# Layer-3 attention: its first chunks prepared in the stage ahead, and the output written by chunk

## The reference

```python
h = silu((n @ w1_w.T) * w1_s) * ((n @ w2_w.T) * w2_s)      # n = layernorm(x)
h = gelu((h @ h1_w.T) * h1_s)
h = gelu((h @ h2_w.T) * h2_s)
x = x + 0.5 * ((h @ w3_w.T) * w3_s)
q, k, v = heads(n @ W_q.T), heads(n @ W_k.T), heads(n @ W_v.T)   # n = layernorm(x), 16 heads of 8
attn = softmax(q @ k.T / sqrt(8))                          # within each batch of 256 tokens
x = x + (attn @ v) @ W_o.T
# and the feed-forward once more
```

## Time and profile before

| what | us |
|---|---|
| three runs | 2952.84 median (2946.71 to 2954.22) |
| the profiled execution | 2956.47 |
| its span | 2954.8 |
| mean granted clock of PE in it | 0.848 of 2.4 GHz |

### The profile page before, as it was taken

One profiled execution on the slowest core, in us unless ns is written; L12 is line 12 of the kernel. 1 busy time (PEld: TensorE's weight loads), 2 busy tenths in 40 slices (PEclk: granted clock), 3 DMA queues, 4 the chain that ended last, 5 costly groups with the idle time before them and its releaser, 6 DMA issues. The chain is left out here.

```text
span 2954.8 us, 44130 instructions
## 1 busy us (share of the span) xinstructions
PE 2255.7 (76%) x13104; PEld 1635.6 (55%) x13105; DVE 1790.6 (61%) x4185; ACT 1048.2 (35%) x2484; POOL 850.4 (29%) x771
## 2 busy tenths in 40 slices
PE   4979959767376732474999951776999699989998
PEld 3645546547364630464666631664877445547777
DVE  5757957573477348841355578725565578855655
ACT  1433315341044101253544412542333156653332
POOL 2544525437404741475000010772000122200000
PEclk9989959965596556798999985997999789989999
DMA  6120011246605567256222263552000233310001
GB/s 209 39 62 1 1 38 39 66 172 133 169 1 179 124 175 143 62 117 146 53 59 52 50 155 61 118 113 70 0 0 0 65 76 94 97 24 1 0 0 29
DMA packets 283584, 221.00 MB, mean 75 GB/s; under 512 B 103072, under 2 KB 254093, under 8 KB 280365
## 3 DMA queue, kind: packets, MB, share of 16 engines
q1 hardware_dynamic: 249261, 185.09, 23.0%
q0 software_dynamic: 34176, 34.09, 7.1%
HBM read 152.98 MB, written 65.17 MB: 74 GB/s over the span
## 5 line engine op out<-in xcount | busy, mean ns | idle before, releaser
L162 POOL TENSOR_TENSOR fields<-ln_t,power 128x4 f32<-128x4 f32 x96 | 98.4, 1051 | 601.0 <-DVE ln_t L155 601.0
L3124 DVE TENSOR_REDUCE s_mx<-s_sa 128x2 f32<-128x512 f32 x256 | 166.6, 686 | 59.8 <-PE s_sa L3277 58.6
L3205 ACT ACTIVATE s_e<-s_sc 128x512 f32<-128x512 f32 x256 | 149.8, 600 | 103.0 <-PE s_sc L3293 100.1
L2860 PE MATMUL s_z<-s_t,s_mix_h 128*128 128x256 f32 x768 | 171.0, 379 | 0.0
L1997 POOL DMA_INDIRECT acc_dram<-s_yo,s_to_i x96 | 152.5, 1588 | 51.8 <-issue 28.1
L1985 POOL DMA_INDIRECT s_xg<-rows_dram,s_from_i x96 | 94.5, 984 | 223.0 <-DVE s_to_i L2118 195.0
L2860 PEld LDWEIGHTS s_z<-s_t,s_mix_h 128*128 128x128 f32 x768 | 145.9, 190 | 19.8
L3277 PE MATMUL s_sa<-s_kx,s_qx 72*128 72x256 bf16 x512 | 110.7, 303 | 26.3 <-DMA s_qx<-q_dram 19.1
L2302 PE MATMUL s_hu<-s_xgt,s_w 128*128 128x128 f32 x768 | 118.6, 301 | 12.4 <-issue 11.5
L191 PE MATMUL s_tp<-ident,xn 128*128 128x128 f32 x192 | 40.3, 347 | 108.0 <-DVE xn L181 106.0
L2906 PE MATMUL s_z<-xnt,s_wt_w 128*128 128x512 f32 x256 | 117.9, 615 | 1.5 <-ACT xnt L197 1.5
(11 more groups left out here) (526 smaller groups left out, 5993.6 us busy)
## 6 DMA issues: line engine op xcount, KB each, us to landing
s_w<-in_L_ffn_W_dram SPq DMA_DIRECT2D x96, 256.0 KB
acc_dram<-s_zero SPq DMA_DIRECT2D x32, 512.0 KB, 5.8
s_share<-share_dram SPq DMA_DIRECT2D x32, 512.0 KB, 6.1
s_kx<-k_dram SPq DMA_DIRECT2D x16, 576.0 KB
s_qx<-q_dram SPq DMA_DIRECT2D x48, 192.0 KB
fields<-acc_dram SPq DMA_DIRECT2D x16, 512.0 KB, 7.5
table_dram<-s_table_rows SPq DMA_DIRECT2D x2, 3136.0 KB, 9.2
s_wg<-in_L_ffn_w_gate_dram SPq DMA_DIRECT2D x64, 96.0 KB
```

Of the source, the lines that this page charges most:

```text
L162: pool.tensor_tensor(core.rstd[:, tiles], core.ln_t[:, 2, tiles], core.power[:, 0:CT], ALU.pow).then_inc(s.scale_ready.sem, 1)
L2860: last = pe.matmul(bank(n)[:, o, :], weights[:, f, o * P:(o + 1) * P], src[:, f, :], start=f == 0, stop=f == HALF - 1)
L3124: dve.tensor_reduce(mx[:, i, t, 2 * pairs:2 * pairs + 2], sa[:, n % 2, :, :], AX.X, ALU.max).then_inc(max_done.sem, 1)
L3205: act.activation(e[:, n % RING, :, :], sc[:, n % 2, :, :], ACT.Exp).then_inc(exp_done.sem, 1)
```

## The change

The parts of layer-3 attention that come ahead of its loop for chunks 0 and 1 go into the first `l3_ffn`, into its last two chunks, 6 and 7 (`first` and unrolled). `early(c, k, at)` is called in each engine's stream between the products of hidden layer k, at point `at`. Chunk 0 of the attention is prepared in chunk 6 (layer 0: scales, normalising, two weights turned, x turned; layer 1: K and Q projections and splitting), chunk 1 in chunk 7 (x turned where the layer norm of a next chunk would be, projections and splitting in layer 0, the last part in layer 1). On PE the two weights are turned after the second product, x after the seventh, K is projected after the third and Q after the sixth product. On ACT the first cut to bf16 follows the first (K) and third (Q) gelu, the second cut the second and fourth. The last of the three parts, and the remainders, are DVE's. PE and ACT use the bank of the layer norm, `s.tp`, and the SBUF of `all_xn`. SP of this stage reads the weights, stores the parts and reads slots 0 and 1, which with the four raw weights (`L3Ahead`) outlive the stage; at its end it waits for all of them.

In the attention the row scores come first. Semaphores of the slots and of the stored parts are preset as if the work had been done there. Chunks 0 and 1 still get their layer norm, for V. The maxima of batch 0 are placed ahead of layer norm, and the 8 row scores of batch 1 are in two halves with V of chunk 0 between them. Three matmuls whose result nobody reads (`warm`) are added, two ahead of the loop and one in batch 0. POOL clears `vz` after two of its eight scales. `warm`, the waits and the order are in the diff.

In the second `l3_ffn` SP writes each chunk of the output as soon as it is added, the statistics of x are not taken, and the stage `end` is gone.

```diff
+class L3Ahead:
+    def __init__(self, s):
+        self.TERMS = 3
+        self.BLOCK = self.TERMS * DH
+        self.ROWS = self.TERMS * self.BLOCK
+        self.ALL_ROWS = self.ROWS + self.TERMS
+        self.NAMES = ("W_q", "W_k", "W_v", "W_o")
+        self.kx = s.sb("kx", [self.ALL_ROWS, 2, HEADS, N], BF16)
+        self.qx = s.sb("qx", [self.ALL_ROWS, 2, HEADS, N], BF16)
+        self.raw = {m: s.sb(f"raw_{m}", [P, P]) for m in self.NAMES}
+def load_operands(eng, core, ahead, slot, kx, qx, sem):
+    eng.dma_start(kx[0:ahead.ROWS, :, :].rearrange("r h t -> r (h t)"),
+                  core.k_dram[slot].rearrange("a d h t -> (a d) (h t)").unsqueeze(1).to_broadcast([ahead.BLOCK, ahead.TERMS, HEADS * N])).then_inc(sem, 16)
+    for a in range(ahead.TERMS):
+        eng.dma_start(qx[a * ahead.BLOCK:(a + 1) * ahead.BLOCK, :, :].rearrange("r h t -> r (h t)"),
+                      core.q_dram[slot].rearrange("d a h t -> (d a) (h t)")).then_inc(sem, 16)
...
+        if first:
+            @block.sync
+            def _(sp):
+                for n, m in enumerate(("W_k", "W_q")):
+                    sp.dma_start(raw_a[n], w[f"L3_attn_{m}"]).then_inc(aw_loaded.sem, 16)
+                for m in ahead.NAMES:
+                    sp.dma_start(ahead.raw[m][:, :], w[f"L3_attn_{m}"]).then_inc(ahead_loaded.sem, 16)
+                for a in range(EARLY):
+                    for n in range(2):
+                        sp.wait_ge(a_split_done.sem, a_split_done.past(2 * a + n))
+                        for i in range(2):
+                            cut = parts[:, n, :, i * N:(i + 1) * N]
+                            if n == 0:
+                                sp.dma_start(core.k_dram[2 * a + i].rearrange("a d h t -> (d h) a t"), cut).then_inc(a_stored[0].sem, 16)
+                            else:
+                                for k in range(TERMS):
+                                    sp.dma_start(core.q_dram[2 * a + i, :, k, :, :], cut[:, k, :]).then_inc(a_stored[1].sem, 16)
+                    if a == 0:
+                        sp.wait_ge(a_stored[0].sem, 32)
+                        sp.wait_ge(a_stored[1].sem, 32 * TERMS)
+                        for i in range(2):
+                            load_operands(sp, core, ahead, i, ahead.kx[:, i, :, :], ahead.qx[:, i, :, :], ahead_loaded.sem)
+                sp.wait_ge(ahead_loaded.sem, 16 * (len(ahead.NAMES) + 2 * (1 + TERMS)))
+                sp.wait_ge(a_stored[0].sem, 32 * EARLY)
+                sp.wait_ge(a_stored[1].sem, 32 * TERMS * EARLY)
...
+        if not first:
+            @block.sync
+            def _(sp):
+                out_rows = core.out.rearrange("b (n p) d -> p (b n) d", p=P)
+                for c in range(CHUNKS):
+                    tiles = slice(c * CT, (c + 1) * CT)
+                    sp.wait_ge(x_added.sem, x_added.past(c))
+                    sp.dma_start(out_rows[:, tiles, :], core.x[:, tiles, :]).then_inc(out_stored.sem, 16)
+                sp.wait_ge(out_stored.sem, 16 * CHUNKS)
...
+            def early_left(a, n):
+                dve.wait_ge(a_first_cut.sem, a_first_cut.past(2 * a + n))
+                dve.scalar_tensor_tensor(left[n], s.tp[:, 0, :], SCALE if n else 1.0, parts[:, n, 0, :],
+                                         ALU.mult, ALU.subtract).then_inc(a_left_ready.sem, 1)
+            def early_last(a, n):
+                dve.wait_ge(a_second_cut.sem, a_second_cut.past(2 * a + n))
+                dve.tensor_tensor(parts[:, n, 2, :], left[n], parts[:, n, 1, :], ALU.subtract).then_inc(a_split_done.sem, 1)
+            def early(c, k, at):
+                if not first or not isinstance(c, int):
+                    return
+                a = c - (CHUNKS - EARLY)
+                if a == 0 and k == 0:
+                    if at == 0:
+                        early_scales()
+                    if at == 3:
+                        early_normal(0, range(2))
+                    if at == 4:
+                        early_normal(0, range(2, CT))
+                if (a, k) in ((0, 1), (1, 0)):
+                    if at == 2:
+                        early_left(a, 0)
+                    if at == 4:
+                        early_last(a, 0)
+                    if at == 5:
+                        early_left(a, 1)
+                if a == 0 and k == 1 and at == 6:
+                    early_last(0, 1)
+                if a == 1 and k == 1 and at == 0:
+                    early_last(1, 1)
...
+                elif first:
+                    early_normal(1)
...
-                dve.wait_ge(x_added.sem, x_added.past(c))
-                new_sums_dve(dve, core, c)
+                if first:
+                    dve.wait_ge(x_added.sem, x_added.past(c))
+                    new_sums_dve(dve, core, c)
...
+            def early_xnt(a):
+                act.wait_ge(a_turned.sem, a_turned.past(a))
+                act.activation(xta, s.tp[:, 0, :], ACT.Copy).then_inc(a_xnt_ready.sem, 1)
+            def early_cut(a, n):
+                act.wait_ge(a_projected.sem, a_projected.past(2 * a + n))
+                if a:
+                    act.wait_ge(a_stored[n].sem, (32, 32 * TERMS)[n] * a)
+                act.activation(parts[:, n, 0, :], s.tp[:, 0, :], ACT.Copy, scale=SCALE if n else 1.0).then_inc(a_first_cut.sem, 1)
+            def early_cut2(a, n):
+                act.wait_ge(a_left_ready.sem, a_left_ready.past(2 * a + n))
+                act.activation(parts[:, n, 1, :], left[n], ACT.Copy).then_inc(a_second_cut.sem, 1)
...
+            def early_turn(a):
+                pe.wait_ge(a_xn_ready.sem, a_xn_ready.past(a))
+                if a:
+                    pe.wait_ge(a_left_ready.sem, a_left_ready.past(2 * a - 1))
+                else:
+                    pe.wait_ge(aw_kept.sem, 1)
+                for j in range(CT):
+                    last = pe.transpose(s.tp[:, 0, j * P:(j + 1) * P], xa[:, j, :], core.ident[:, :])
+                last.then_inc(a_turned.sem, 1)
+            def early_project(a, n):
+                if n:
+                    pe.wait_ge(a_left_ready.sem, a_left_ready.past(2 * a))
+                else:
+                    pe.wait_ge(a_xnt_ready.sem, a_xnt_ready.past(a))
+                pe.matmul(s.tp[:, 0, :], wt_a[n], xta, start=True, stop=True).then_inc(a_projected.sem, 1)
...
-        parts_stored = [s.sig(f"parts_stored{n}", (32, 96)[n]) for n in range(2)]
-        kq_loaded = [s.sig(f"kq_loaded{n}") for n in range(SLOTS)]
+        parts_stored = [s.sig(f"parts_stored{n}", 3 * (32, 96)[n]) for n in range(2)]
+        kq_loaded = [s.sig(f"kq_loaded{n}", (64, 64, 0, 0)[n]) for n in range(SLOTS)]
...
             sp.wait_ge(ones_ready.sem, 1)
-            sp.dma_start(kx[ROWS:ALL_ROWS, :, :, :].rearrange("p u h t -> p (u h t)").rearrange("p (n t) -> p n t", t=CW),
-                         ones[:, :].unsqueeze(1).to_broadcast([TERMS, SLOTS * HEADS * N // CW, CW])).then_inc(ones_loaded.sem, 16)
-            store(0, 0)
-            load(0, 0, 0, False)
-            load(0, 0, 1, False)
-            store(1, 1)
+            for part in (ahead.kx, kx_more):
+                sp.dma_start(part[ROWS:ALL_ROWS, :, :, :].rearrange("p u h t -> p (u h t)").rearrange("p (n t) -> p n t", t=CW),
+                             ones[:, :].unsqueeze(1).to_broadcast([TERMS, 2 * HEADS * N // CW, CW])).then_inc(ones_loaded.sem, 16)
             load(1, 1, 0, False)
             place_nm(0, 0, 0)
...
-            ln_scales_pool(pool, core, s)
-            pool.wait_ge(s.xn_ready.sem, s.xn_ready.past(1))
+            ln_scales_pool(pool, core, s, range(2))
             pool.memset(vz[:, :, :, :, :], 0.0).then_inc(v_clear.sem, 1)
             pool.wait_ge(v_clear.sem, 1)
             pool.memset(vz[:, :, :, :, DH:HW].rearrange("p u j h c -> p (u j h) c"), 1.0).then_inc(v_clear.sem, 1)
             pool.memset(zero[:, :], 0.0).then_inc(v_clear.sem, 1)
             pool.wait_ge(v_clear.sem, 3)
+            ln_scales_pool(pool, core, s, range(2, CHUNKS))
...
+            ln_scales_dve(dve, core, s)
             dve.memset(ones[:, :], 1.0).then_inc(ones_ready.sem, 1)
             dve.memset(m3[:, :, :, TERMS:, :], 0.0)
             dve.tensor_copy(ident_b[:, :], core.ident[:, :]).then_inc(ident_ready.sem, 1)
-            ln_scales_dve(dve, core, s)
-            ln_dve(dve, core, s, 0, 0)
-            ln_dve(dve, core, s, 1, 1)
-            split(0, 0)
-            split(0, 1)
-            split(1, 0)
-            split(1, 1)
-            dve.wait_ge(v_clear.sem, 2)
-            keep_v(0, 0)
             for n in range(STEPS):
                 largest(0, 0, n)
             split_maxima(0)
-            for n in range(LEAD):
+            ln_dve(dve, core, s, 0, 0)
+            for n in range(LEAD // 2):
+                largest(1, 1, n)
+            dve.wait_ge(v_clear.sem, 2)
+            keep_v(0, 0)
+            ln_dve(dve, core, s, 1, 1)
+            for n in range(LEAD // 2, LEAD):
...
+            keep_nm(0, 0)
```

(51 more changed lines are left out.)

189 lines of the change are left out of this document (138 added, 51 removed).

## The result

The median went from 2952.75 us (2946.71 to 2954.22) to 2911.47 us (four runs, 2906.64 to 2916.07): 41.3 us less where 29.6 were forecast. The ratio with its 95% interval, which is not that of the two medians, is 0.9872 [0.985, 0.9893], some 38 us. Two further measurements of the unchanged pair gave 0.9877 [0.9854, 0.9899] and 0.99 [0.9871, 0.9928].

A forecast was written before the change was run, and what follows sets the result against it. PE was taken to bound the feed-forward stage and the attention loop, at a low clock in batch 0. Terms summed to -29.6 us: 2956.5 to 2926.9, less 3.6 for the median, 2923 us; 8-in-10 range 2908 to 2940.

The forecast's parts named there:

- Preparation in chunks 6 and 7: First layer-3 feed-forward stage: added projections and transposes on PE cost +4.6 us (4.6 to 9); DVE and ACT work hidden.
- Rival B: Feed-forward stage ahead pays more, by early steps waiting or an end waiting for stores: up to +8, 2931 us; chance 0.12.
- Stage start: Start of attention: three more SP semaphore increments ahead of the barrier cost +0.2 us (0 to 0.4).
- The prologue: Attention ahead of its loop: first matmul at T + 30.5 instead of T + 50.6, -20.1 us (-22 to -16).
- The row's bound of +3.5: Attention prologue: POOL's memset might hold DVE's maxima, as it held a CAST; bounds 0 and +3.5 us, 0 taken.
- Batch 0: First 16 loop steps of attention: clock raised by warm matmuls, 16 us against 24.05, -8.0 us (-9.2 to +1.7).
- Rival A: Attention loop: the clock stays low through batch 0, whose term becomes +1.7, total 2933 us; chance 0.17.
- The wait for slot 0's second load: Attention loop: PE's wait for chunk 2's operands grows from 1.34 to 2.2 us, +0.9 (0 to 4).
- The output: Tail: stores by chunk leave only a last 256 KB store, landing at 2947.2 instead of 2954.4, -7.2 us (-8 to -5).
- rival C: Attention loop, chunk 6: no fall of the clock after the load wait, 9 us less, 2914 us; chance 0.15.

The follow-up runs named there:

- norm_first: Changed kernel with layer norm of both chunks and chunk 0's V product put back ahead of the maxima: 2911.26 us, ratio 0.9872 to the kernel before.
- no_warm: Changed kernel without its three warm matmuls: 2920.68 us, ratio 0.9907 to the kernel before.
- before_warm: Kernel before with only the three warm matmuls added: 2939.67 us, ratio 0.9964 to the unchanged kernel before.
- before_out: Kernel before with only the output part of the change (stores by chunk, no last statistics, no stage `end`): 2944.26 us, ratio 0.9978.
- both: Changed kernel with Q parts stored as split, row scores and maxima moved forward, one warm matmul ahead of the loop: 2908.11 us, ratio 0.9857 to before.

## Why the prediction was right, point by point

- **Preparation in chunks 6 and 7** (+4.6): +4.5 over the two chunks. Over the whole stage it is 294.9 to 296.6 us in the ten executions with this code against 290.8 to 291.4 in the four without, +4.5 between the means. None of the hand-overs cost anything, and the stage end did not wait for SP: its reads were issued at 2280.9 to 2285.7, 28 us before the end of the last addition, its last stores 6.8 us before. Rival B did not come.
- **Stage start** (+0.2): the gap is 1.67 against 1.64 us. The sum left out the gap ahead of the second feed-forward stage, which went from 1.17 to 1.58; it is part of "the rest".
- **The prologue** (-20.1): -20.3, with the maxima at T + 2.1 and the loop at T + 30.26. T + 30.5 was taken between two sums, T + 31 with the warm matmuls at the low clock and T + 29 with the clock up; the clock was still low, and the work ahead of them 0.7 shorter than summed. The memset held nothing: 13 maxima took 9.05 us, 0.696 each, against the 0.69 of the earlier trace rows. The row's bound of +3.5, from the CAST, did not apply to a reduction from PSUM. The Trainium skill's "SBUF — State Buffer" ("Who interferes with whom") names no reduction among the operations that can take the shared port pair, and the trace agrees. norm_first adds what the sum had not separated: only 1.8 of these 20 us are the order.
- **Batch 0** (-8.0): -8.7. Two microseconds were taken as low; it was 0.9 (2346.6 to 2347.5). no_warm and before_warm, one from each side, confirm the cause: 23.55 without the warm matmuls, 15.06 with them. Rival A did not come.
- **The wait for slot 0's second load** (+0.9): here the step failed. The prediction had PE's way get 0.9 shorter and the chain from K's projection to the landing keep its length. But that 0.9 is the K projection itself, which stands in both. The first cut on POOL, which follows it, before and after:

```profile
2394.21 1.04 POOL L3090 TENSOR_TENSOR s_parts<-s_proj,s_zero 128x512 bf16<-128x512 f32 x1 [60.73 <-ACT s_proj L3200]
...
2362.27 1.04 POOL L3324 TENSOR_TENSOR s_parts<-s_proj,s_zero 128x512 bf16<-128x512 f32 x1 [32.86 <-ACT s_proj L3421]
```

It starts 3.64 us after K's projection did, and now 2.54: 1.1 of the chain went with the clock. The whole chain was 2420.32 - 2390.57 = 29.75 and is 2387.70 - 2359.73 = 27.97, 1.8 shorter, PE's own way 1.4 shorter, and so the wait went from 1.34 to 1.00 instead of to 2.2. Q's projection took 1.02 both times. Over all executions the sign is not settled: the wait is 1.00, 1.16 and 1.72 after, and 1.34 and 0.54 before. One row was no basis for a size here.
- **The output** (-7.2): -7.6, and -7.6 alone in before_out. The store of 256 KB lands in 2.3 us, where 2.5 was worked out.
- **The median.** The sum by stage, taken between executions without a fall, is -32.4 against -29.6; of the 2.8 us between them 1.3 lie in the rest of the loop (-0.4 for +0.9), the others are 0.6 and less. The first medians differ by 41.3, the later ones by 34.7 (0.9877) and 31.2 (0.99). The forecast's ratio, 2923 / 2952.84 = 0.9899, lies just outside the first interval, at the edge of the second and inside the third. So the size was forecast too small for the first measurement, and the time lies in the range because the range had room for rival C. What the medians have beyond -32.4 can be the falls, and the unchanged stages ahead, which take 2020 to 2028 us; the medians cannot tell them apart. The prediction gave rival C, no fall in chunk 6, a chance of 0.15 and the value 2914, taking the fall for a trait of the kernel before that could or could not survive. That 2914 lies near the measured 2911 is luck: the runs show a chance event at each load wait, in either kernel. C's size was right (9 us for 20 us at the low clock; 10 measured). What it lacked was that the new kernel can fall as well.

Not settled: why the kernel after was 7.0 us earlier at the first feed-forward stage in the first execution. The same point lies at 2025.4 in the second execution of the kernel before, at 2025.2 and 2025.1 in two of the kernel after, and at 2020.3 in both; the code ahead is the same, and I did not follow it up.

## What to carry to other kernels

When a stage begins with work that needs only data known earlier, look for room in the stage ahead on the engines that do not bound it, and count only what the bounding engine has to issue: here 4 us there bought 20. Then look at the granted clock of the first busy stretch: three full-width f32 matmuls whose result nobody reads were worth 5 to 6 us net, in the old kernel (8.9 - 2.5) as in the new one (8.2 - 2.9). And before a difference of 10 us is explained, profile the same kernel twice; short waits of PE on a DMA can each be followed by a spell at the low clock: at the two paces of the earlier trace rows a spell of 7 us costs 3 and one of 20 us some 9, here behind waits of 1.5 to 2 us.
